# Per-image statistics from four 32-row products, a later load of the second image, and four fewer warm-up products

## The reference

```
x = x + net(gn(x))          # gn: per image and channel, 32 groups of 1 channel
gn(v)  = (v - mean) / sqrt(var + 1e-5)          # mean, var over the 64x64 pixels
block(x, w1, w2, stride, ds) =
    relu(conv3(relu(conv3(x, w1, stride)*S), w2)*S + (conv1x1(x, ds)*S or x))
net: e0b0, e0b1 (64x64) -> e1b0, e1b1 (32x32) -> e2b0, e2b1 (16x16)
     -> relu(deconv)*S + f1 -> relu(deconv)*S + f0      # S = 1/sqrt(1.001)
```

## Time and profile before

| | before |
|---|---|
| median of 3 runs | 89.10 us (89.04 to 89.35) |
| profiled execution | 89.06 us |
| its span | 87.3 us |
| PE busy | 80.4 us, 92% of the span |
| DVE / ACT / POOL busy | 56.6 / 43.8 / 25.6 us |
| start of the first convolution's products | 8.29 us into the span |

### The profile page before, as it was taken

How to read it: one execution, slowest core, us unless ns; L and a number is a source line. 1 busy time by engine, 2 the same in 40 slices (tenths; PEclk the granted TensorE clock), 3 DMA queues, 4 the chain that set the end, 5 groups by cost and what they waited for, 6 DMA issues and landing times.

```text
span 87.3 us, 1464 instructions
## 1 busy us (share of the span) xinstructions
PE 80.4 (92%) x509; PEld 72.0 (83%) x509; DVE 56.6 (65%) x166; ACT 43.8 (50%) x94; POOL 25.6 (29%) x39
## 2 busy tenths in 40 slices
PE   5999999999999999999999999999999999799700
PEld 3777999998778889999988777999999999587500
DVE  5569999799968696522223567999697877213450
ACT  6005214679555047455530239799999996001300
POOL 7200052799960000444452000100289100000330
PEclk9999999999999999999999999999999999999995
DMA  1979930023475106640000000000000000000075
GB/s 27 247 238 274 315 131 0 0 56 108 153 211 204 30 0 173 188 128 0 0 0 0 0 0 4 0 0 0 0 8 0 0 0 0 0 0 8 4 274 207
DMA packets 4183, 6.51 MB, mean 75 GB/s; under 512 B 464, under 2 KB 2128, under 8 KB 4176
## 3 DMA queue, kind: packets, MB, share of 16 engines
q1 hardware_dynamic: 4032, 6.29, 23.5%
q10 hardware_dynamic: 144, 0.13, 0.5%
HBM read 5.37 MB, written 1.05 MB: 74 GB/s over the span
## 4 chain that ended last, share of the span: by engine, by line
PE 91%; DVE 3%; issue 1%; DVEq 0%
PE psum L843 79%; PE psum L870 8%; DVE result L834 2%; PE psum L1023 1%; PE psum L886 1%; PE psum L863 1%; PE psum L1068 1%; PE psum L879 1%; DVE odd L756 0%; DVEq L175 0%; DVE last L754 0%; DVE flat L752 0%; DVE zeros L678 0%; DVEq L833 0%; DVE eps L680 0%
## 5 line engine op out<-in xcount | busy, mean ns | idle before, releaser
L498 POOL TENSOR_TENSOR odd<-relu,odd 128x363 fp32r<-128x363 f32 x12 | 13.6, 1150 | 15.4 <-ACT odd L563 15.4
L843 PE MATMUL psum<-shared,w_e0b0c 128*128 128x364 f32 x72 | 12.5, 331 | 0.0
L773 DVE SCALAR_TENSOR_TENSOR relu<-psum,inside 128x363 f32<-128x363 f32 (+1 forms) x16 | 8.1, 510 | 6.5 <-PE psum L843 5.1
L843 PEld LDWEIGHTS psum<-shared,w_e0b0c 128*128 128x128 f32 x72 | 12.0, 188 | 0.3 <-issue 0.3
L843 PE MATMUL psum<-shared,w_e0b1c 128*128 128x364 f32 x72 | 12.1, 328 | 0.0
L843 PEld LDWEIGHTS psum<-shared,w_e0b1c 128*128 128x128 f32 x72 | 12.0, 188 | 0.1
L843 PE MATMUL psum<-odd,w_e0b0c 128*128 128x512 f32 x48 | 11.6, 400 | 0.0
L843 PE MATMUL psum<-odd,w_e0b1c 128*128 128x512 f32 x48 | 11.6, 400 | 0.0
L843 PEld LDWEIGHTS psum<-odd,w_e0b1c 128*128 128x128 f32 x48 | 9.1, 189 | 2.2
L843 PEld LDWEIGHTS psum<-odd,w_e0b0c 128*128 128x128 f32 x48 | 9.1, 189 | 2.2
L563 ACT ACTIVATE odd<-relu 128x363 fp32r<-128x363 f32 x12 | 6.1, 507 | 7.2 <-DVE relu L773 7.2
(11 more groups left out here) (125 smaller groups left out, 126.2 us busy)
## 6 DMA issues: line engine op xcount, KB each, us to landing
x_sb<-x_in SPq DMA_DIRECT2D x4, 160.0 KB, 3.8
raw<-e0b0c_in SPq DMA_DIRECT2D x2, 256.0 KB, 4.8
raw<-e0b1c_in SPq DMA_DIRECT2D x2, 256.0 KB, 5.0
raw<-e1b1c_in SPq DMA_DIRECT2D x2, 256.0 KB, 3.2
raw<-e2b1c_in SPq DMA_DIRECT2D x2, 256.0 KB, 2.7
raw<-e1b0c_in SPq DMA_DIRECT2D x1, 448.0 KB, 3.7
raw<-e2b0c_in SPq DMA_DIRECT2D x1, 448.0 KB, 3.9
x_sb<-x_in SPq DMA_DIRECT2D x2, 192.0 KB, 4.0
```

The source lines that it names most:

```text
L498: pool.tensor_tensor(split_of(piece, 1), fp32_of(piece), split_of(piece, 0).bitcast(F32), ALU.subtract).then_inc(lo_ready, 1)
L773: last = dve.scalar_tensor_tensor(out=target, in0=sums, scalar=0.0, in1=mask, op0=ALU.max, op1=ALU.mult)
L843: last = pe.matmul(target, w, moving, start=(first and n == 0), stop=(final and n == len(terms) - 1), skip_group_check=skip)
```

## The change

Image 0's statistics are summed without the masked copies. Each of four products takes 32 partitions (one position q) of `same_channel` and of the 18 values, and writes 18 columns into a bank of its own, banks 4 to 7; `bn_aggr` reads 18 values from each of the four. Image 1's statistics are made as before. SP waits, before it issues image 1's x, until image 0's last range has landed. The first group of zero products has 18 in place of 22, and they write bank 3.

```diff
-WARM_UP = [22, 14]
+WARM_UP = [18, 14]
+STATS_BANKS = [4, 5, 6, 7]
@@ SP
                 if k == 0:
+                    sp.wait_ge(x_loaded[0][-1], 16)
                     load_x(1)
@@ DVE, add_stats
+                if image == 0:
+                    last.then_inc(stats_ready, 1)
+                    return
                 step(last)
                 dve.tensor_tensor(spread[:, image], stats..., quad_mask..., ALU.mult).then_inc(stats_spread, 1)
@@ DVE, norm
-                dve.bn_aggr(moments[:, image], psum[:, BANKS - 1, 0:4 * VALUES]).then_inc(moments_ready, 1)
+                first_bank, values = (BANKS - 1, 4 * VALUES) if image else (STATS_BANKS[0], VALUES)
+                dve.bn_aggr(moments[:, image], psum[:, first_bank:BANKS, 0:values]).then_inc(moments_ready, 1)
@@ PE, sum_stats
-                pe.wait_ge(stats_spread, image + 1)
                 pe.wait_ge(const_loaded, 16)
+                if image == 0:
+                    pe.wait_ge(stats_ready, 1)
+                    for q in range(4):
+                        of_q = slice(CH * q, CH * q + CH)
+                        last = pe.matmul(psum[:, STATS_BANKS[q], 0:VALUES], same_channel[of_q, 0:P], stats[of_q, image],
+                                         start=True, stop=True)
+                    last.then_inc(stats_summed, 1)
+                    return
+                pe.wait_ge(stats_spread, 1)
                 pe.matmul(psum[:, BANKS - 1, 0:4 * VALUES], ...)
@@ PE
-            def warm_up(count, bank=BANKS - 2):
+            def warm_up(count, bank=STATS_BANKS[0] - 1):
```

More of the change, by code:

```diff
@@ L236, in build @@
         norm_step = sem("norm_step")
+        stats_ready = sem("stats_ready")
         stats_spread = sem("stats_spread")
```

## The result

| | before | changed |
|---|---|---|
| median | 89.00 us (88.81 to 89.35, 20 runs) | 88.47 us (88.18 to 90.16, 20 runs) |
| ratio, with its 95% interval | | 0.9942 (0.9922 to 0.9962) |
| profiled execution | 89.06 us | 88.36 us |
| its span | 87.3 us | 86.6 us |
| first convolution product | 8.29 us | 7.85 us |

By this ratio the changed kernel is 0.58% faster. So the range held, and the likeliest case was not what came.

A forecast was written before the change was run, and what follows sets the result against it. PE's chain up to the first convolution product was taken to bound the kernel: 8.29 - 8.03 = 0.26 gained, so 87.28 - 0.26 + 1.78 = 88.8 us profiled, median 88.85. The range was 88.45 to 90.3.

The forecast's parts named there:

- the likeliest case: Whole kernel: median 88.85 us, own range 88.5 to 89.1, no change that can be told; chance 0.52.
- What bounds the kernel: PE's chain: bringing the first convolution product (8.29 us) forward brings the end forward equally, if other engines keep up.
- Part 1: Image 0's statistics on DVE: without masked copies PE's weight load comes at 5.35 in place of 5.61, 0.26 gained.
- Part 2: Statistics' products on PE: four 32-row products take 0.70 to `bn_aggr` in place of 0.74, 0.04 gained.
- Part 3: Zero products on PE: 18 end at 4.9, PE stands 0.45, clock rises at 7.0, the 14 end at 8.0.
- rival 3: Start on PE: clock already up at the statistics' products, first convolution product at 7.7 to 7.8, 88.5 us; chance 0.08.
- Part 4: First convolution product on PE: at 8.03 in place of 8.29, held by weights rounded on ACT and by zero products.
- the sum: First convolution product: comes forward from 8.29 to 8.03, 0.26 in all.
- Part 5: Image 1's x behind SP's wait: last range lands 8.85 to 9.25, before DVE wants it at 9.34; costs nothing.
- Rival 2: Image 1's x lands late, at 10.55; PE stands some 0.5 and the gain is gone: 89.1 to 89.8; chance 0.08.
- Rival 1: PE's break delays the clock's rise, slow zero products hold PE: 90.0 for a rise at 9.4, 91.2 at 11.9; chance 0.32.

The follow-up runs named there:

- E6: E1 plus two tiny DVE memsets ahead of image 0's statistics, 199 DVE instructions: 88.89 us, ratio 0.9979.
- E2: The kernel before with 18 zero products in the first group in place of 22, nothing else: 89.57 us, ratio 1.0002.
- E4: The kernel before with only SP's wait ahead of image 1's x added: 89.21 us, ratio 1.0006.
- E1: The changed kernel with 20 zero products in the first group in place of 18: 88.59 us, ratio 0.9943.
- E3: E1 without SP's wait ahead of image 1's x: 88.68 us, ratio 0.9950.
- E5: E1 plus one tiny DVE memset ahead of image 0's statistics: 88.54 us, ratio 0.9930.
- E7: The changed kernel with 20 zero products ahead of the statistics' products and 10 behind, in place of 18 and 14: 88.52 us, ratio 0.9943.
- E8: The changed kernel with 16 zero products in the first group in place of 18: 89.56 us, ratio 0.9998.
- E10: The changed kernel with 22 zero products in the first group, as in the kernel before: 88.69 us, ratio 0.9950.
- E12: The changed kernel run once more without any edit: 89.60 us, ratio 0.9960.
- E9: E1 plus two tiny DVE memsets behind image 0's statistics, 200 DVE instructions: 88.66 us, ratio 0.9946.
- E11: E9 with 21 zero products ahead of the statistics' products and 11 behind, in place of 20 and 14: 88.69 us, ratio 0.9945.

## Why the prediction was right in its range and wrong in its case

**What bounds the kernel.** Right for PE, wrong in the step from PE to the end. The first convolution product came 0.44 forward, and the whole stretch up to 79.4 us with it, by 0.47: the chain's 346 products took their 60.23 us again, with no new stop in this profile (E6's has one). But I wrote "Whatever brings the first convolution product (8.29 us) forward brings the end forward by as much, as long as the other engines keep up". That took the tail as fixed, and it is the premise that failed. DVE's instruction stream became one instruction shorter and the tail went from 1.66 to 1.36. The lengths of all fourteen profiles bear this out: 199 gave 1.66 (before, E2, E4, E6), 198 gave 1.36 or 1.37 (changed, E1, E3, E5, E7, E8, E10, E12), 200 gave 1.30 (E9, E11). In time it is E6's 88.89 against E1's 88.59, or against E7's 88.52 on E6's own chip. I had read DVE's removed copy as work and not as a place in a stream.

**Part 1, no copies.** 0.20 measured, 0.26 forecast. The weight load came 0.11 after the statistics, not 0.06. Small and in direction right. It was 0.12 in E3, and 0.20 in E1, where the zeros ran until then.

**Part 2, four products for one.** At the slow level 0.70 (E1, E5) or 0.72 (E12), as taken, against 0.74 for the single product. At the fast level 0.50 (changed, E3, E6 and others), where the single product took 0.48 (E4). So four products cost what one does within 0.04, at either level; the 0.24 that the profiled execution gained here is the clock's, not the products'. `bn_aggr` kept its 0.48 over four banks.

The Trainium skill, "TensorEngine Tiling (Array Packing)", Key Properties, says that a change of mode drains the engine. The zero products behind the change back began at 5.79, when the four had been begun from 5.44, and `bn_aggr` could start 0.13 later, so the change back cost the statistics nothing. Whether the zero products had to wait for a drain these rows don't tell, and no run was made that would price it by itself.

**Part 3, the zero products.** I had worked out a stop of 0.45, from the end of 18 spacings at 4.9; by that measure it was 0.53 in the changed kernel's profile and 0.47 in E12's. The trace counts from the end of the last zero product's record, 5.10, and so gives 0.35 and 0.29. The rise of the clock at 7.0 was taken from one execution, and it isn't a constant: it came at 3.8 to 7.0 in twelve of the fourteen profiles and at 9.4 and 10.2 in two, which both have 18 zeros ahead (E12 and E2). The step "if the clock rises at 7.0 as before" failed: the changed kernel's profile has it by 5.5, where the first of the four products took 0.28 and not E12's 0.36. That was rival 3's case.

**Part 4, the first product.** 8.03 forecast; 7.85 in the profiled execution, 8.08 in E1 with the statistics' products at the slow level, as I had assumed them, and with 20 zeros, which hold them 0.1 longer. Rival 3 had said 7.7 to 7.8. The 0.26 of the sum was 0.21 in E1 and 0.44 in the changed kernel's profile, and to each came some 0.3 from the tail.

**Part 5, image 1's x.** Forecast 8.85 to 9.25; its last range landed at 9.10, and DVE took image 1's statistics from 8.34 without idling for it. The weights landed at 6.16 where I had said about 6. ACT took them at 6.64. The groups by line of the changed kernel, last range of image 1's x and then the weights:

```profile
L448 SPq DMA_DIRECT2D x_sb<-x_in x1: 432/432/432, 5.6 to 5.6; - x1
...
DMA to landing us min/median/max: 3.5/3.5/3.5
...
L456 SPq DMA_DIRECT2D raw<-e0b0c_in x1: 432/432/432, 2.6 to 2.6; - x1
...
DMA to landing us min/median/max: 3.6/3.6/3.6
```

Rival 2 did not occur here, but it did in E6's profile, where that range landed at 9.63 and PE lost 0.35. I had called 9.34 the latest time that costs nothing. In E9's and E11's the range landed at 9.49 and 9.66 and DVE idled 0.10 and 0.06 for it, and PE lost 0.04 at most. In the medians the wait costs nothing that E4 could tell, in a kernel whose image 1 is wanted later.

**Rival 1, the clock rises later.** It is real. I had given it 0.32, as one way in which the median could go. It befalls single executions: 12 of the 29 runs of the changed kernel lie above 89.0, where the clock was seen late in the one of them that has a profile (E12). The count goes with the zeros: none of 11 with 22 (E10), and none of the 108 of before and 12 of E4, which have 22 too; 5 of 59 over 89.9 with 20 (two in E5, three in E9, none in E1, E3, E6 and E7, whose highest is 89.10); 12 of 29 with 18, and 6 of 12 in E2; 9 of 12 with 16. E11, with 21, has 3 of 12, more than its place in this order.

Is it the break? In six profiles PE stood 0.16 to 0.94 ahead of the statistics' products after the clock had risen (E3, E4, E6, E8, E10, E11), and it stayed up. In the two late ones it stood 0.29 and 0.53 while the clock was low; but the changed kernel's 0.35 began at the low level too, and there the clock was up by 5.5. So if it is the break, it is one before the rise, and in some executions only. But no run parts the break from the number of zeros: both changed together, and fewer products ahead might do the same without a break. That the break is the cause is argued, not shown. That 20 and 21 show any has a possible cause that I have not shown either: image 0's x lands later in some executions (5.00 in E4's profile against 4.73; the statistics end at 5.64 in E11's, with a break of 0.37), which reopens the break. There is another reading: all eight of these runs are in kernels with an added `memset` (E5, E9, E11; none of E6's 12), while none of the 29 runs of E1, E3 and E7, which have none, is over 89.01; and the chips differ too. No run parts these. The price was right. I had 90.0 for a rise at 9.4; less the 0.3 of the tail, which I didn't know of, that is 89.7, and E12's execution with a rise at 9.4 took 89.62. The groups by line of E12, on PE, show both halves of it, 14 slow zero products, and convolution products that are slow at first and become quick only later:

```profile
L885 PE MATMUL psum<-zeros x14: 394/421/421, 5.9 to 8.7; 128*128 128x256 bf16 x14
...
L850 PE MATMUL psum<-shared,w_e0b0c x2: 405/529/653, 8.8 to 9.2; 128*128 128x364 f32 x2
...
L850 PE MATMUL psum<-shared,w_e0b0c x11: 322/329/405, 9.2 to 11.0; 128*128 128x364 f32 x11
```

The Trainium skill, "TensorE: Matmul & The Clock Gate", Part 1, says that the point of release varies from run to run. The fourteen profiles agree, 3.8 to 10.2. What E8 and E10 add is that a kernel's own zeros and break go with how often it comes late.

**So the change's parts are worth this.** Summing without copies: 0.2 (E6 against before, 0.05 to 0.32 by its interval; 0.21 in E1's trace). The shorter stream, which nobody wrote into the diff: 0.3 (E1 against E6). The wait on SP: nothing measurable by itself. The cut from 22 to 18 zeros: in an execution with an early rise nothing, since the profiles of the changed kernel and of E10 have PE's and DVE's ends at the same times, and their 88.36 and 88.59 differ only behind DVE's last result. Over the runs it is at best 0.1: the changed kernel's lower thirteen are 0.59 under before's median on their chip, E10 0.50 on its own, and E12's lower four there have a median of 88.65 against E10's 88.69. Against that, 1.2 is lost in two executions of five. E10 keeps the rest and leaves the cut out. The mean of its runs is 88.71, that of the changed kernel's 20 and 9 runs 88.82 and 89.33, that of before on E10's and E12's chip 89.17. By the median the changed kernel is ahead in one comparison (88.47) and behind in the other (89.60). For regular use I would take E10, or E1 by its median of 88.59.

## What to carry to other kernels

Before adding a saving at the start to the end, look at how the last instructions of each engine are issued: an "issue" of 0.4 us in the tail's chain can come or go with one instruction more or less anywhere ahead of it. When the first products of a kernel cover the rise of the clock, don't read its time from one profile, and don't trim them without a count of runs: count the runs of each cluster and not only the median. When trimming brings 0.1 at best and a second cluster with it, leave it.

## What the runs showed of the hardware that I had not expected

- DVE halts for 0.41 us ahead of an instruction late in its stream, the 192nd recorded one in all fourteen profiles. With 199 instructions in the trace that is the first result, where nothing hides it; with 198 it is the second, behind a running one, and costs 0.06 (results 0.40 apart, not 0.34); with 200 it costs nothing there that the trace shows. Why DVE halts at that place no run shows.
- A `memset` put ahead of a waiting instruction can take over that wait, and leaves the length of the stream as it was (E5). To set a length one has to count semaphore waits too.
- Four 32-row products with 18 columns each, into four banks, cost as much to their reader as one product with 72 columns: 0.50 and 0.48 at the fast level, 0.70 to 0.72 and 0.74 at the slow one.
- The clock's rise came at 3.8 to 7.0 us into the span in twelve profiles, and at 9.4 and 10.2 in two. By the run times it is late in about 12 of 29 executions with 18 zero products ahead and a break of some 0.3 us behind them, in 9 of 12 with 16, and in none of 11 with 22. Whether the break or the number of products does it, no run shows. A break of up to 0.94 us after the rise did not bring the clock down (six profiles).
